# First cross attention: numerator and denominator of a head in one 32-column product, divided and projected in another layout

## The chip, the cores and the metric

The kernel runs on one core of a Trainium2 chip. The metric is device time in microseconds for one launch of the whole program, which computes a small two-layer network; the change touches its first stage only. The stationary operand of a TensorE product is loaded by a weight load (PEld), the moving operand is then streamed by the matmul (PE). VectorE is DVE, ScalarE is ACT, GpSimd is POOL and SyncE, which issues the transfers, is SP.

## The reference

Only the first of the six steps matters here. `x` is normalised (8 samples of 64 tokens, 256 features), and attends to 1024 context rows of 256 features per sample, with 16 heads of 16 features:

```python
rq = (iQ @ Wq.T).reshape(b, q, H, ADIM)          # 8 x 64 x 16 x 16
kv = (iK @ Wkv.T).reshape(b, s, 2, H, ADIM)      # 8 x 1024 x 2 x 16 x 16
scores = einsum('bqhd,bshd->bhqs', rq, rk) / sqrt(ADIM)
scores = where(mask[:, None, :, :], -1e32, scores)
t = relu(scores + nbias[0]); t = t * t
attn = t / (t.sum(-1, keepdims=True) + 1e-32)
o = einsum('bhqs,bshd->bqhd', attn, rv).reshape(b, q, H * ADIM)
x = x + o @ Wo.T
```

The division is made after the product with the values: a numerator (squares times values) over a denominator (sum of the squares).

## The kernel before

`xattn0` writes one instruction stream for each engine; waits on semaphores tie them together, and each engine works through its own list in order. The loop runs over 8 samples `b`, and in each over 4 values of `j`, each with two of the eight 128-row tiles `k` of the context; `n = 8b + k` counts tiles.

TensorE does in one pass of the loop over `j`, in this order: `scores` of the two tiles after the next (`n + 2`, `n + 3`; L468, four 32-row strips of the array side by side), `outputs` of `n` and `n + 1`, and two `piece`s of the keys and values of sample `b + 1` (L181, three fp32r products for one fp32 product). In the last sample there are no pieces. In `outputs` a tile's squares, transposed already (`pr`: context row by (r, c, head of a pair, token)), stream past 32 columns of values, that is two heads (L485, eight matmuls of 128 columns), so that half of each result is the product of one head's squares with the other head's values and is not wanted; and then past 32 columns of ones (L489, four matmuls of 256 columns), which gives the sums. Four matmuls at a time write the four 32-partition quarters of a bank. Each fp32 matmul shows as two matmul records and two weight loads in the trace.

VectorE clamps the scores of a tile (`clamp`, L378), and ScalarE squares them (`squares`, L318), evicts the pieces (`evict`, L307 and L311) and splits the next context (`split`, L298), whose low part GpSimd computes (L286). `scores` of tiles `n + 2`, `n + 3` wait until `clamp` of the pair before has read the same banks. `normalize(b - 1)` on VectorE stands behind the two clamps of `j == 0`: it picks the wanted halves with a 0/1 mask over partitions (`pairmask`, L388 to L392), takes the reciprocal (L394) and multiplies (L395). `limits` and `queries` of the next sample stand at `j == 1` (L366, L368, L361). After the last sample TensorE waits for all of `oT` and does the output projection (L523, eight matmuls), and VectorE adds it to `x` (L428). At the start GpSimd builds the constants, and TensorE waits for `const` before its 20 warming matmuls (L100), which precede the first piece.

```python
pe.wait_ge(const, 3)
core.warm(7, 20)
pe.wait_ge(w_lo, 1)
for n in range(4):
    piece(0, n)
```

Of the kernel before, what the change touches and what calls it, by code (L numbers as in the profile page):

```python
# [188 lines left out]
def xattn0(core, x_d, ctxT_d, maskT_d, wqT_d, wkvT_d, woT_d, nbias_d):  # L189
# [8 lines left out]
    with ExitStack() as ctx:  # L198
# [5 lines left out]
        wo = sb("wo", [P, DC, D])  # L204
# [5 lines left out]
        v = [sb(f"v{i}", [P, KT, D]) for i in range(2)]  # L210
        ones = sb("ones", [P, 32])
# [13 lines left out]
        part, den = sb("part", [P, DC, T]), sb("den", [P, DC, T])  # L225
        num, den_part = sb("num", [P, DC, T]), sb("den_part", [P, DC, T])
        oT = sb("oT", [P, DC, B, T])
# [9 lines left out]
        s_psum, u_ready, p_ready, pv = sem("s_psum"), sem("u_ready"), sem("p_ready"), sem("pv")  # L237
        o_ready, y_psum, x_out = sem("o_ready"), sem("y_psum"), sem("x_out")
# [5 lines left out]
        @block.sync  # L244
        def _(sp):
            def load_context(b):
                for c in range(DC):
                    sp.dma_start(ctxT[:, c, :], ctxT_d[b, c * P:(c + 1) * P, :]).then_inc(ctx_in[c], 16)

            def load_mask(b):  # L250
                sp.dma_start(mask_u8[:], maskT_d[b, :, :].rearrange("p (k t) -> p k t", t=T)).then_inc(mask_in, 16)

            sp.dma_start(wkv[:], wkvT_d.rearrange("(c p) o -> p c o", p=P)).then_inc(wkv_in, 16)
            load_context(0)
            sp.dma_start(x[:], x_d.rearrange("(j p) d -> p j d", p=P)).then_inc(x_in, 16)
# [3 lines left out]
            sp.dma_start(wo[:], woT_d.rearrange("(c p) o -> p c o", p=P)).then_inc(w_in, 16)  # L259
            for b in range(1, B):  # L260
                sp.wait_ge(hi_ready, DC * b)
                sp.wait_ge(lo_ready, DC * b)
                load_context(b)
                sp.wait_ge(mask_read, b)
                load_mask(b)

        @block.gpsimd
        def _(pool):
# [13 lines left out]
            g.memset(ones[:], 1.0).then_inc(const, 1)  # L282
# [7 lines left out]
        def _(act):  # L290
# [9 lines left out]
            def evict(b, n):  # L300
                act.wait_ge(kv_psum, PIECES * b + n + 1)
                bank = core.bank(4 + n % 2)
                if n < 4:
                    c, h = n % 2, n // 2
                    if b >= 2:
                        act.wait_ge(s_psum, KT * (b - 1))
                    A.copy(kT[b % 2][:, c, 512 * h:512 * h + 512], bank).then_inc(kv_ready, 1)  # L307
                else:
                    if b >= 2:
                        act.wait_ge(pv, KT * (b - 1))  # L310
                    A.copy(v[b % 2][:, 2 * (n - 4):2 * (n - 4) + 2, :],  # L311
                           bank.rearrange("p (k d) -> p k d", k=2)).then_inc(kv_ready, 1)
# [24 lines left out]
            act.wait_ge(w_in, 48)  # L337
            squares(0)
            squares(1)
            for b in range(B):  # L340
                for j in range(KT // 2):
                    for i in range(2):
                        n = KT * b + 2 * j + 2 + i
                        if n < LAST:
                            squares(n)
                    if b + 1 < B:
                        evict(b + 1, 2 * j)
                        evict(b + 1, 2 * j + 1)
                    if j == 1 and b + 2 < B:
                        split(b + 2)  # L350

        @block.vector
        def _(dve):
# [29 lines left out]
            def normalize(b):  # L383
                dve.wait_ge(pv, KT * (b + 1))
                half = lambda i: core.bank(6 + b % 2)[:, 256 * i:256 * i + 256].rearrange(
                    "p (c g t) -> p c g t", c=DC, g=2)
                o, d = half(0), half(1)
                step(V.tensor_scalar(part[:], o[:, :, 1, :], pairmask[:, 1:2], None, ALU.mult), False)  # L388
                step(V.tensor_scalar(den_part[:], d[:, :, 1, :], pairmask[:, 1:2], 1e-32, ALU.mult, ALU.add))
                step(V.scalar_tensor_tensor(num[:], o[:, :, 0, :], pairmask[:, 0:1], part[:], ALU.mult,  # L390
                                            ALU.add), False)
                step(V.scalar_tensor_tensor(den[:], d[:, :, 0, :], pairmask[:, 0:1], den_part[:], ALU.mult,  # L392
                                            ALU.add))
                step(V.reciprocal(den[:], den[:]))  # L394
                V.tensor_tensor(oT[:, :, b, :], num[:], den[:], ALU.mult).then_inc(o_ready, 1)  # L395
# [10 lines left out]
            dve.wait_ge(w_in, 48)  # L406
            step(V.tensor_scalar(floor[:], nb[:], -float(HD ** 0.5), None, ALU.mult))
            limits(0)
            dve.wait_ge(const, 3)
# [4 lines left out]
            for b in range(B):  # L414
                for j in range(KT // 2):
# [4 lines left out]
                    if j == 0 and b > 0:  # L420
                        normalize(b - 1)
# [4 lines left out]
            for j in range(2):  # L426
                dve.wait_ge(y_psum, j + 1)
                V.tensor_tensor(x[:, 2 * j:2 * j + 2, :], x[:, 2 * j:2 * j + 2, :],  # L428
                                core.bank(2 + j).rearrange("p (j d) -> p j d", d=D), ALU.add).then_inc(x_out, 1)

        @block.tensor
        def _(pe):
# [40 lines left out]
            def outputs(n):  # L473
                b, k = n // KT, n % KT
                bank = core.bank(6 + b % 2)
                prob = pr[:, n % NP, :].rearrange("p (r c n) -> p r c n", r=RT, c=DC)
# [24 lines left out]
            pe.wait_ge(w_in, 48)  # L501
# [7 lines left out]
            for b in range(B):  # L509
                for j in range(KT // 2):  # L510
# [10 lines left out]
            for j in range(TT):  # L521
                for c in range(DC):
                    last = t.matmul(core.bank(2 + j // 2)[:, D * (j % 2):D * (j % 2) + D],  # L523
                                    oT[:, c, 2 * j:2 * j + 2, :].rearrange("p b q -> p (b q)"), wo[:, c, :],
                                    start=c == 0, stop=c == DC - 1)
                if j % 2:
                    last.then_inc(y_psum, 1)
# [1393 lines left out]
def layout(inputs):  # L1921
# [8 lines left out]
    for n in ("Wq", "Wkv", "Wo"):  # L1930
        a["L0_xattn_" + n] = a["L0_xattn_" + n].T

# [25 lines left out]
```

## Time and profile before

| | |
|---|---|
| median of 3 runs | 1226.44 us (1224.24 to 1230.47) |
| the profiled execution, its own time | 1229.6 us |
| its span | 1227.9 us |
| busy in the span: PE, PEld | 1109.2 us (90%), 930.3 us (76%) |
| busy in the span: DVE, ACT, POOL | 613.6, 578.8, 283.2 us |
| the first cross attention | from 0 to 225 us of the span |

A row of the timeline view has a start and a duration in microseconds, engine, line, operation, tiles and a count of merged records; what stands in square brackets is the engine's idle time before it, and who ended it. Matmul records overlap, so where a merged row's next row starts tells more than its duration.

### The profile page before, as it was taken

To read this page: it belongs to the slowest core of one execution; us is meant where nothing else is said; L and a number is where in the kernel's file an instruction comes from. 1 tells how busy PE (TensorE), PEld (TensorE's weight loads), DVE (VectorE), ACT (ScalarE), POOL (GpSimd) and SP (SyncE) were. 2 spreads that over 40 slices of the span, in tenths; PEclk is the share of its full clock that TensorE was granted. 3 is DMA by queue.
4 is the path that set the end of the run, shared out by engine and by line. 5 is a ranking of instruction groups with operands and counts; after the bars stand their busy time and mean duration, and the time that the engine had idled before them with its cause. 6 is when DMAs were issued, how large, how long until landed. Compare 5 with 4: busy or idle time off the path is not lost. (4 is left out here: it accounts for less than half of the span.)

```text
span 1227.9 us, 21490 instructions
## 1 busy us (share of the span) xinstructions
PE 1109.2 (90%) x8708; PEld 930.3 (76%) x8708; DVE 613.6 (50%) x863; ACT 578.8 (47%) x779; POOL 283.2 (23%) x195
## 2 busy tenths in 40 slices
PE   7999998737899987999999999999999967999998
PEld 6778876434589954798898989889886546888887
DVE  3565566587444435555555555555541266334333
ACT  4666665312366625444444444444430323665563
POOL 2112110205124412111302111131200340343341
PEclk9999999968699978999999999999999977999999
DMA  4111100101023230111112111113000402233220
GB/s 152 45 39 41 72 5 2 39 1 56 1 86 94 60 137 9 60 35 35 35 34 68 34 34 34 34 34 102 0 1 1 152 0 70 69 102 102 68 68 18
DMA packets 47453, 62.39 MB, mean 51 GB/s; under 512 B 5457, under 2 KB 37665, under 8 KB 47393
## 3 DMA queue, kind: packets, MB, share of 16 engines
q1 hardware_dynamic: 47392, 61.52, 15.6%
q8 instruction: 46, 0.75, 0.3%
q14 instruction: 15, 0.12, 0.0%
HBM read 60.99 MB, written 0.52 MB: 50 GB/s over the span
## 5 line engine op out<-in xcount | busy, mean ns | idle before, releaser
L1487 ACT ACTIVATE f_pr<-ps,f_negmax 128x1024 f32<-128x1024 f32 x64 | 71.4, 1116 | 178.8 <-DVE f_negmax L1554 178.8
L181 PE MATMUL ps<-f_pT_hi,f_cN_hi 128*128 128x256 f32 x512 | 145.5, 284 | 2.4 <-DVE f_pT_lo L1549 2.4
L181 PE MATMUL ps<-f_pT_hi,f_cN_lo 128*128 128x256 f32 x512 | 145.0, 283 | 0.0
L181 PE MATMUL ps<-f_pT_lo,f_cN_hi 128*128 128x256 f32 x512 | 144.9, 283 | 0.0
L1549 DVE TENSOR_TENSOR f_pT_lo<-ps,f_pT_hi 128x1024 fp32r<-128x1024 f32 x64 | 78.2, 1222 | 78.7 <-ACT f_pT_hi L1495 78.7
L378 DVE SCALAR_TENSOR_TENSOR a_u<-ps,a_floor,a_cap 128x1024 f32<-128x1024 f32 x64 | 79.2, 1279 | 74.8 <-PE ps L468 74.8
L181 PE MATMUL ps<-e_cT_hi,f_qb_hi 128*128 128x512 f32 x256 | 106.2, 415 | 8.0 <-POOL e_cT_lo L1449 8.0
L959 DVE TENSOR_TENSOR k_h_lo<-k_h,k_h_hi 128x512 fp32r<-128x512 f32 x64 | 58.6, 924 | 101.1 <-ACT k_h_hi L940 101.0
L893 POOL TENSOR_TENSOR k_w_lo<-k_w,k_w_hi 128x1024 fp32r<-128x1024 f32 x32 | 76.5, 2396 | 121.5 <-ACT k_w_hi L920 121.5
L181 PEld LDWEIGHTS ps<-f_pT_hi,f_cN_hi 128*128 128x128 f32 x512 | 98.0, 191 | 4.8 <-DVE f_pT_lo L1549 2.6
L181 PE MATMUL ps<-e_cT_hi,f_qb_lo 128*128 128x512 f32 x256 | 101.1, 395 | 0.0
L181 PE MATMUL ps<-e_cT_lo,f_qb_hi 128*128 128x512 f32 x256 | 100.6, 393 | 0.0
L181 PEld LDWEIGHTS ps<-f_pT_lo,f_cN_hi 128*128 128x128 f32 x512 | 98.1, 192 | 1.6
L318 ACT ACTIVATE a_pr<-a_u,a_nb 128x1024 f32<-128x1024 f32 x64 | 73.7, 1152 | 51.8 <-DVE a_u L378 50.5
L181 PEld LDWEIGHTS ps<-f_pT_hi,f_cN_lo 128*128 128x128 f32 x512 | 98.0, 191 | 0.0
L1554 DVE TENSOR_REDUCE f_negmax<-ps 128x1 f32<-128x1024 f32 x64 | 78.0, 1219 | 36.8 <-PE ps L181 36.8
L1449 POOL TENSOR_TENSOR e_cT_lo<-e_rawT,e_cT_hi 128x512 fp32r<-128x512 f32 x32 | 42.3, 1355 | 220.3 <-ACT e_cT_hi L1471 193.5
L1495 ACT CAST f_pT_hi<-ps 128x1024 fp32r<-128x1024 f32 x64 | 64.8, 1013 | 54.0 <-PE ps L1607 54.0
L936 ACT ACTIVATE k_h<-ps,k_b 128x512 f32<-128x512 f32 x64 | 44.0, 688 | 72.4 <-PE ps L181 72.4
L1607 PE MATMUL ps<-ident,f_pr 128*128 128x128 f32 x512 | 66.6, 273 | 12.6 <-DVE f_pT_lo L1549 11.8
L181 PE MATMUL ps<-k_w_hi,k_h_hi 128*128 128x256 f32 x256 | 73.2, 286 | 0.5 <-DVE k_h_lo L959 0.3
L181 PE MATMUL ps<-k_w_hi,k_h_lo 128*128 128x256 f32 x256 | 72.5, 283 | 0.0
(325 smaller groups left out, 2660.5 us busy)
## 6 DMA issues: line engine op xcount, KB each, us to landing
k_w<-in_L_ffn_W SPq DMA_DIRECT2D x32, 512.0 KB, 3.7
a_ctxT<-in_ctxT SPq DMA_DIRECT2D x16, 512.0 KB, 4.4
d_w<-in_L_ffn_w SPq DMA_DIRECT2D x32, 256.0 KB, 2.7
e_rawT<-in_ctxT SPq DMA_DIRECT2D x8, 1024.0 KB, 4.9
e_raw<-in_ctx SPq DMA_DIRECT2D x8, 1024.0 KB, 5.5
e_wk<-in_L_xattn_w_k SPq DMA_DIRECT2D x1, 1024.0 KB, 6.7
e_wq<-in_L_xattn_w_q SPq DMA_DIRECT2D x1, 1024.0 KB, 8.8
g_wv<-in_L_xattn_w_v SPq DMA_DIRECT2D x1, 1024.0 KB, 7.8
```

Source lines behind the costliest of these rows:

```text
L181: last = nc.tensor.matmul(out, a[i], b[j], start=start and n == 0, stop=stop and n == 2, skip_group_check=skip)
L318: A.activation(pr[:, n % NP, :], u[:, n % NU, :], ACT.Square, bias=nb[:], scale=HD ** -0.5).then_inc(p_ready, 1)
L378: V.scalar_tensor_tensor(u[:, n % NU, :].rearrange("p (r w) -> p r w", r=RT), core.psum[:, 0:2048].rearrange("p (r w) -> p r w", r=RT)[:, ...
L893: self.c.nc.gpsimd.tensor_tensor(lo[:], raw[:], hi[:].bitcast(F32), ALU.subtract).then_inc(self.lo[i], 1)
L936: A.activation(self.h[:, f % self.RH, :], self.c.bank(f % 4), self.func, bias=bias).then_inc(self.h_ready, 1)
L959: V.tensor_tensor(self.hp[1][:, f % self.RG, :], self.h[:, f % self.RH, :], self.hp[0][:, f % self.RG, :].bitcast(F32), ALU.subtract).then ...
L1449: nc.gpsimd.tensor_tensor(cT[1][:, c, cols], rawT[:, c, cols], cT[0][:, c, cols].bitcast(F32), ALU.subtract).then_inc(t_lo, 1)
L1487: nc.scalar.activation(pr[:, p % NPR, :], core.ps[p % 2][:], ACT.Exp, bias=negmax[:, p:p + 1], accum_out=total[:, p:p + 1]).then_inc(exp_r ...
L1495: nc.scalar.copy(pT[0][:, g, :, P * (p % 2):P * (p % 2) + P], core.ps[2][:].rearrange("p (k n) -> p k n", n=P)).then_inc(pT_hi, 1)
L1549: nc.vector.tensor_tensor(pT[1][:, g, :, cols], core.ps[2][:].rearrange("p (k n) -> p k n", n=P), pT[0][:, g, :, cols].bitcast(F32), ALU.s ...
L1554: nc.vector.tensor_reduce(negmax[:, p:p + 1], core.ps[p % 2][:], AX, ALU.max, negate=True).then_inc(max_ready, 1)
L1607: last = nc.tensor.transpose(core.ps[2][:, k * P:(k + 1) * P], pr[:, p % NPR, k * P:(k + 1) * P], core.ident[:])
```

## The change

- `v` holds, per head, 16 columns of values and 16 columns of ones. `outputs` does one matmul of 64 columns per head against these 32 columns (16 matmuls a tile, four at a time). In each 32-partition quarter of the bank 16 partitions then hold numerators and 16 hold the sum, 16 times over. The matmuls against `ones` are gone.
- `numerators` (ScalarE, at `j == 0` of the next sample, ahead of the squares) copies the sample's 128x256 result out of PSUM. `denominators` (TensorE, behind `outputs` of `j == 0`) multiplies it by the 0/1 matrix `spread`, which puts each head's sum beside its numerators, into the other half of the bank. `normalize`, now behind the clamps of `j == 1`, adds 1e-32, takes the reciprocal and multiplies, all of 256 columns.
- `oT` and `wo` have 4 slices of 128 partitions in place of 2, with zero rows in `wo` where `oT` holds no numerators. The projection is 16 matmuls in place of 8. Three of its four row blocks (`project(0)` to `project(2)`) stand in the last sample's loop, where there are no pieces.
- GpSimd fills `spread`, all of `wo` and the ones columns of both `v` buffers at the start, and TensorE and VectorE wait for `const` 6 in place of 3. `wo` is loaded by four transfers behind a wait for its fill. The squares and the products with `Wq` no longer wait for `wo`.

```diff
-        wo = sb("wo", [P, DC, D])
+        wo = sb("wo", [P, 4, D])
...
-        v = [sb(f"v{i}", [P, KT, D]) for i in range(2)]
-        ones = sb("ones", [P, 32])
+        v = [sb(f"v{i}", [P, KT, H, 2 * HD]) for i in range(2)]
+        spread = sb("spread", [P, 4, 32])
...
+            sp.wait_ge(const, 4)
+            for j in range(4):
+                sp.dma_start(wo[32 * j:32 * j + HD, :, :], woT_d[HD * j:HD * j + HD, :].rearrange(
+                    "d (i o) -> d i o", o=D)).then_inc(wo_in, 16)
...
-            g.memset(ones[:], 1.0).then_inc(const, 1)
+            step(g.memset(spread[:], 0.0))
+            g.affine_select(out=spread[:], in_=spread[:], compare_op=ALU.not_equal, fill=1.0, base=-HD,
+                            pattern=[[-32, 4], [0, 32]], channel_multiplier=1).then_inc(const, 1)
+            g.memset(wo[:], 0.0).then_inc(const, 1)
+            for i in range(2):
+                g.memset(v[i][:, :, :, HD:2 * HD], 1.0).then_inc(const, 1)
...
+            def numerators(b):
+                act.wait_ge(pv, KT * (b + 1))
+                if b >= 1:
+                    act.wait_ge(o_ready, b)
+                A.copy(num[:], core.bank(6 + b % 2)[:, 0:256].rearrange("p (h t) -> p h t", t=T)
+                       ).then_inc(num_ready, 1)
...
+                    if j == 0 and b > 0:
+                        numerators(b - 1)
...
-                dve.wait_ge(pv, KT * (b + 1))
...
+                dve.wait_ge(den_psum, b + 1)
+                step(V.tensor_scalar(den[:], core.bank(6 + b % 2)[:, 256:512].rearrange("p (h t) -> p h t", t=T), 1e-32,
+                                     None, ALU.add))
                 step(V.reciprocal(den[:], den[:]))
                 V.tensor_tensor(oT[:, :, b, :], num[:], den[:], ALU.mult).then_inc(o_ready, 1)
...
-            dve.wait_ge(const, 3)
+            dve.wait_ge(const, 6)
...
-                    if j == 0 and b > 0:
+                    if j == 1 and b > 0:
                         normalize(b - 1)
...
                 for c in range(DC):
-                    for j in range(4):
-                        quarter = slice(32 * j, 32 * j + 32)
-                        t.matmul(bank[quarter, P * c:P * c + P], v[b % 2][:, k, P * c + 32 * j:P * c + 32 * j + 32],
-                                 prob[:, j, c, :], start=k == 0 and c == 0, stop=k == KT - 1,
-                                 skip_group_check=True)
-                for j in range(4):
-                    last = t.matmul(bank[32 * j:32 * j + 32, 2 * P:4 * P], ones[:],
-                                    prob[:, j, :, :].rearrange("p c n -> p (c n)"), start=False, stop=k == KT - 1, skip_group_check=True)
+                    for g in range(2):
+                        col = T * (2 * c + g)
+                        for j in range(4):
+                            last = t.matmul(bank[32 * j:32 * j + 32, col:col + T], v[b % 2][:, k, 8 * c + 2 * j + g, :],
+                                            prob[:, j, c, g, :], start=k == 0 and c == 0 and g == 0,
+                                            stop=k == KT - 1, skip_group_check=True)
                 last.then_inc(pv, 1)
 
-            pe.wait_ge(const, 3)
+            def denominators(b):
+                pe.wait_ge(num_ready, b + 1)
+                t.matmul(core.bank(6 + b % 2)[:, 256:512], spread[:].rearrange("p j m -> p (j m)"),
+                         num[:].rearrange("p h t -> p (h t)"), start=True, stop=True).then_inc(den_psum, 1)
+
+            def project(j):
+                pe.wait_ge(o_ready, 2 * j + 2)
+                for i in range(4):
+                    last = t.matmul(core.bank(4 + j // 2)[:, D * (j % 2):D * (j % 2) + D],
+                                    oT[:, i, 2 * j:2 * j + 2, :].rearrange("p b q -> p (b q)"), wo[:, i, :],
+                                    start=i == 0, stop=i == 3)
...
+            pe.wait_ge(const, 6)
             core.warm(7, 20)
...
+                    if j == 0 and b > 0:
+                        denominators(b - 1)
                     if b + 1 < B:
                         piece(b + 1, 2 * j)
                         piece(b + 1, 2 * j + 1)
-            pe.wait_ge(o_ready, B)
...
+                    else:
+                        if j == 0:
+                            pe.wait_ge(wo_in, 64)
+                            pe.wait_ge(kv_ready, PIECES * B)
+                        if j < 3:
+                            project(j)
+            denominators(B - 1)
+            project(TT - 1)
```

TensorE at `j == 0` of the second sample (`b = 1`), before, from the scores to the first pieces:

```order
L468 MATMUL ps<-a_qd,a_kT 128x128 x16
L485 MATMUL ps<-a_pr,a_v 32x128 x8
L489 MATMUL ps<-a_pr,a_ones 32x256 x4
L485 MATMUL ps<-a_pr,a_v 32x128 x8
L489 MATMUL ps<-a_pr,a_ones 32x256 x4
L181 MATMUL ps<-a_ctx_hi,a_wkv_hi 128x512
```

The same place in the changed kernel, where L479 is the line of the scores, L497 that of the products of a head and L504 that of the product with `spread`:

```order
L181 MATMUL ps<-a_wkv_hi,a_ctx_lo 128x256
L479 MATMUL ps<-a_qd,a_kT 128x128 x16
L497 MATMUL ps<-a_pr,a_v 32x64 x32
L504 MATMUL ps<-a_num,a_spread 128x256
L181 MATMUL ps<-a_ctx_hi,a_wkv_hi 128x512
```

24 matmuls of 128 and 256 columns have become 32 of 64, and one product of 256 columns stands between them and the pieces.

VectorE in the same sample before, from the clamps of `j == 2` of the sample ahead to those of `j == 2` of this one, where `normalize` stands between the clamps of `j == 0` and of `j == 1`:

```order
L378 SCALAR_TENSOR_TENSOR a_u<-ps,a_floor,a_cap 128x1024 x6
L388 TENSOR_SCALAR a_part<-ps,a_pairmask 128x128
L389 TENSOR_SCALAR a_den_part<-ps,a_pairmask 128x128
L390 SCALAR_TENSOR_TENSOR a_num<-ps,a_pairmask,a_part 128x128
L392 SCALAR_TENSOR_TENSOR a_den<-ps,a_pairmask,a_den_part 128x128
L394 RECIPROCAL a_den<-a_den 128x128
L395 TENSOR_TENSOR a_oT<-a_num,a_den 128x2x64
L378 SCALAR_TENSOR_TENSOR a_u<-ps,a_floor,a_cap 128x1024 x2
L366 TENSOR_SCALAR a_big<-a_mask_u 128x512
L368 TENSOR_SCALAR a_cap<-a_big,a_floor 128x2048
L361 TENSOR_TENSOR a_qd<-a_qT,a_pairmask 128x128 x2
```

And in the changed kernel:

```order
L396 SCALAR_TENSOR_TENSOR a_u<-ps,a_floor,a_cap 128x1024 x8
L403 TENSOR_SCALAR a_den<-ps 128x256
L405 RECIPROCAL a_den<-a_den 128x256
L406 TENSOR_TENSOR a_oT<-a_num,a_den 128x4x64
L384 TENSOR_SCALAR a_big<-a_mask_u 128x512
L386 TENSOR_SCALAR a_cap<-a_big,a_floor 128x2048
L379 TENSOR_TENSOR a_qd<-a_qT,a_pairmask 128x128 x2
```

The six instructions of `normalize` have become three of twice the width, and they, `limits` and `queries` now form one block without a clamp between.

TensorE at the end of the changed stage, in the last sample (L510 is the line of `project`; before, all of the projection stood behind the last `outputs`):

```order
L479 MATMUL ps<-a_qd,a_kT 128x128 x16
L497 MATMUL ps<-a_pr,a_v 32x64 x32
L504 MATMUL ps<-a_num,a_spread 128x256
L510 MATMUL ps<-a_wo,a_oT 128x256 x4
L479 MATMUL ps<-a_qd,a_kT 128x128 x16
L497 MATMUL ps<-a_pr,a_v 32x64 x32
L510 MATMUL ps<-a_wo,a_oT 128x256 x4
```

A quarter of the projection, four matmuls, follows the products of each of `j` 0 to 2.

## Rows read from the trace of the kernel before

**Rows 1.** Busy time of each engine, PEclk granted, in two stretches of the stage

```profile
100.00:150.00 50.00, 50.00 (x856) 40.27 (x852) 29.86 (x38) 30.88 (x37) 9.53 (x5) 1.00 0.14 49
...
220.00:222.00 2.00, 2.00 (x7) 1.56 (x6) 0.63 (x1) 0.00 (x0) 0.00 (x0) 0.51 0.00 0
```

**Rows 2.** Groups of the stage by form: count, busy us, mean ns of one

```profile
L485 PE MATMUL ps<-a_pr,a_v 128*32 128x128 f32 x1024 | 41.0, 278 | 0.8 <-ACT a_pr L318 0.7
L489 PE MATMUL ps<-a_pr,a_ones 128*32 128x256 f32 x512 | 39.8, 383 | 0.0
```

**Rows 3.** Timeline of PE, one pass of the loop over j (sample 3)

```profile
101.12 0.61 PE L489 MATMUL ps<-a_pr,a_ones 128*32 128x256 f32 x8
101.55 0.62 PE L485 MATMUL ps<-a_pr,a_v 128*32 128x128 f32 x16
101.99 0.61 PE L489 MATMUL ps<-a_pr,a_ones 128*32 128x256 f32 x8
102.53 0.38 PE L181 MATMUL ps<-a_wkv_hi,a_ctx_hi 128*128 128x256 f32 x1
...
105.57 1.17 PE L468 MATMUL ps<-a_qd,a_kT 32*128 32x128 f32 x32
```

**Rows 4.** Timeline of DVE, one sample and the clamps behind it

```profile
106.81 2.48 DVE L378 SCALAR_TENSOR_TENSOR a_u<-ps,a_floor,a_cap 128x1024 f32<-128x1024 f32 x2 [3.54 <-PE ps L468]
109.20 0.34 DVE L388 TENSOR_SCALAR a_part<-ps,a_pairmask 128x128 f32<-128x128 f32 x1
...
112.78 2.48 DVE L378 SCALAR_TENSOR_TENSOR a_u<-ps,a_floor,a_cap 128x1024 f32<-128x1024 f32 x2 [1.02 <-PE ps L468]
115.17 0.42 DVE L366 TENSOR_SCALAR a_big<-a_mask_u 128x512 f32<-128x512 uint8 x1
...
116.83 0.48 DVE L361 TENSOR_TENSOR a_qd<-a_qT,a_pairmask 128x128 f32<-128x128 f32 x2
118.75 2.48 DVE L378 SCALAR_TENSOR_TENSOR a_u<-ps,a_floor,a_cap 128x1024 f32<-128x1024 f32 x2 [1.44 <-PE ps L468]
```

**Rows 5.** Timeline of ACT, the squares in the first pass of the same sample

```profile
108.13 2.35 ACT L318 ACTIVATE a_pr<-a_u,a_nb 128x1024 f32<-128x1024 f32 x2 [1.87 <-DVE a_u L378]
```

**Rows 6.** Timeline of PE, later stages: products of 16 and of 8 columns

```profile
306.52 1.66 PE L1277 MATMUL ps<-c_vd,c_pT 128*64 128x16 f32 x29 [1.10 <-ACT c_pT L1187]
...
337.15 1.92 PE L819 MATMUL ps<-d_gate_w,c_mlaT 128*128 128x8 f32 x16 [1.04 <-PEq L1110]
```

**Rows 7.** Groups of DVE, ACT and POOL by form, as prices

```profile
L394 DVE RECIPROCAL a_den<-a_den 128x128 f32<-128x128 f32 x8 | 7.6, 953 | 0.3
L1219 DVE RECIPROCAL c_sm<-c_sm 128x16 f32<-128x16 f32 x4 | 1.0, 253 | 0.1
L1841 DVE TENSOR_TENSOR h_y<-ps,h_bo 128x256 f32<-128x256 f32 x4 | 1.6, 424 | 2.2 <-PE ps L1888 2.2
L307 ACT COPY a_kT<-ps 128x512 f32<-128x512 f32 x32 | 18.5, 578 | 15.1 <-PE ps L181 15.1
L1157 POOL MEMSET c_vd<- 128x1024 f32 x1 | 1.0, 951 | 0.0
L286 POOL TENSOR_TENSOR a_ctx_lo<-a_ctxT,a_ctx_hi 128x1024 fp32r<-128x1024 f32 x14 | 33.2, 2394 | 136.0 <-ACT a_ctx_hi L298 136.0
```

**Rows 8.** Timeline of PE and DVE, the last sample and the projection

```profile
201.41 1.17 PE L468 MATMUL ps<-a_qd,a_kT 32*128 32x128 f32 x32
...
215.00 0.64 PE L485 MATMUL ps<-a_pr,a_v 128*32 128x128 f32 x16
...
216.14 0.35 DVE L388 TENSOR_SCALAR a_part<-ps,a_pairmask 128x128 f32<-128x128 f32 x1 [2.38 <-PE ps L489]
...
218.76 5.41 PE L523 MATMUL ps<-a_wo,a_oT 128*128 128x256 f32 x16 [2.69 <-DVE a_oT L395]
...
224.21 0.69 DVE L428 TENSOR_TENSOR resid<-resid,ps 128x512 f32<-128x512 f32 x1 [2.15 <-PE ps L523]
```

**Rows 9.** Timeline of PE, the start of the program

```profile
2.78 7.40 PE L100 MATMUL ps<-ident 128*128 128x128 f32 x40 [2.78 <-POOL a_ones L282]
9.94 0.48 PE L181 MATMUL ps<-a_ctx_hi,a_wkv_hi 128*128 128x512 f32 x1
```

More of the change, by code:

```diff
@@ L224, in xattn0 @@
         pr = sb("pr", [P, NP, H * T])
-        part, den = sb("part", [P, DC, T]), sb("den", [P, DC, T])
-        num, den_part = sb("num", [P, DC, T]), sb("den_part", [P, DC, T])
-        oT = sb("oT", [P, DC, B, T])
+        num, den = sb("num", [P, 4, T]), sb("den", [P, 4, T])
+        oT = sb("oT", [P, 4, B, T])
         x_in, wkv_in, w_in, const = sem("x_in"), sem("wkv_in"), sem("w_in"), sem("const")
@@ L237, in xattn0 @@
         s_psum, u_ready, p_ready, pv = sem("s_psum"), sem("u_ready"), sem("p_ready"), sem("pv")
+        num_ready, den_psum, wo_in = sem("num_ready"), sem("den_psum"), sem("wo_in")
         o_ready, y_psum, x_out = sem("o_ready"), sem("y_psum"), sem("x_out")
@@ L310, in evict @@
                         act.wait_ge(pv, KT * (b - 1))
-                    A.copy(v[b % 2][:, 2 * (n - 4):2 * (n - 4) + 2, :],
-                           bank.rearrange("p (k d) -> p k d", k=2)).then_inc(kv_ready, 1)
+                    A.copy(v[b % 2][:, 2 * (n - 4):2 * (n - 4) + 2, :, 0:HD],
+                           bank.rearrange("p (k h d) -> p k h d", k=2, h=H)).then_inc(kv_ready, 1)
+            def numerators(b):
[4 more added lines that the diff above has]
+                       ).then_inc(num_ready, 1)
             def squares(n):
@@ L336, in _ @@
                 A.copy(qT[:, c, :], core.bank(2 + c)).then_inc(q_ready, 1)
-            act.wait_ge(w_in, 48)
+            act.wait_ge(w_in, 32)
             squares(0)
@@ L350, in _ @@
                         split(b + 2)
+            numerators(B - 1)
         @block.vector
@@ L383, in normalize @@
             def normalize(b):
-                dve.wait_ge(pv, KT * (b + 1))
[L385 to L393, printed above, removed]
+                dve.wait_ge(den_psum, b + 1)
+                step(V.tensor_scalar(den[:], core.bank(6 + b % 2)[:, 256:512].rearrange("p (h t) -> p h t", t=T), 1e-32,
+                                     None, ALU.add))
                 step(V.reciprocal(den[:], den[:]))
@@ L482, in outputs @@
                 for c in range(DC):
-                    for j in range(4):
-                        quarter = slice(32 * j, 32 * j + 32)
-                        t.matmul(bank[quarter, P * c:P * c + P], v[b % 2][:, k, P * c + 32 * j:P * c + 32 * j + 32],
-                                 prob[:, j, c, :], start=k == 0 and c == 0, stop=k == KT - 1,
-                                 skip_group_check=True)
-                for j in range(4):
-                    last = t.matmul(bank[32 * j:32 * j + 32, 2 * P:4 * P], ones[:],
-                                    prob[:, j, :, :].rearrange("p c n -> p (c n)"), start=False, stop=k == KT - 1, skip_group_check=True)
-                last.then_inc(pv, 1)
-            pe.wait_ge(const, 3)
+                    for g in range(2):
[4 more added lines that the diff above has]
+                                            stop=k == KT - 1, skip_group_check=True)
+                last.then_inc(pv, 1)
+            def denominators(b):
[8 more added lines that the diff above has]
+                                    start=i == 0, stop=i == 3)
+                if j % 2:
+                    last.then_inc(y_psum, 1)
+            pe.wait_ge(const, 6)
             core.warm(7, 20)
@@ L500, in _ @@
                 piece(0, n)
-            pe.wait_ge(w_in, 48)
+            pe.wait_ge(w_in, 32)
             for c in range(DC):
@@ L519, in _ @@
                         piece(b + 1, 2 * j + 1)
-            pe.wait_ge(o_ready, B)
[L521 to L527, printed above, removed]
+                    else:
[6 more added lines that the diff above has]
+            project(TT - 1)
 def store_x(core, out_d):
@@ L1929, in layout @@
     a["maskT"] = mask.reshape(B, T, KT, P).transpose(0, 3, 2, 1).reshape(B, P, KT * T)
-    for n in ("Wq", "Wkv", "Wo"):
+    for n in ("Wq", "Wkv"):
         a["L0_xattn_" + n] = a["L0_xattn_" + n].T
+    a["L0_xattn_Wo"] = a["L0_xattn_Wo"].T.reshape(2, 4, 2, 16, D).transpose(1, 3, 0, 2, 4).reshape(64, 4 * D)
     a["L0_ffn_q_w"] = a["L0_ffn_q_w"].reshape(D, 16, 2, 8)[:, :, 0, :].reshape(D, P)
```

7 lines of the change are left out of this document (3 added, 4 removed).

## Prediction

> **What bounds the kernel now.** I read first the busy times by stretch: between 100 and 150 us TensorE is busy all of 50.00 us at a granted clock of 1.00, VectorE 29.86 and ScalarE 30.88 us [rows 1]. So in the loop every column that TensorE no longer streams is time, until another engine's loop becomes longer. The timeline shows one pass of the loop over j [rows 3]: the two tiles' products go 0.43 us (ones), 0.44 us (values), and so on, and the next scores start at 105.57. The clamps of neighbouring passes start 5.97 us apart [rows 4], and of the four passes of a sample two hold key pieces and two value pieces; I take 5.97 for the first and second pass and 6.01 for the other two (scores at 105.57, 6.01 behind those of the pass before, by the same pattern). A sample takes 23.96 us. VectorE's slack is seen in the square brackets: it waits 3.54 us for the scores ahead of the clamps of a first pass, but only 1.02 behind normalize and 1.44 behind limits and queries [rows 4]. It has slack in each pass, and little in two of them.
>
> **Products of a tile.** Matmuls of 128 and of 256 columns take 278 and 383 ns [rows 2]: 105 ns for 128 columns, 0.82 ns a column. 16 records of the values take 0.44 us [rows 3], that is four rounds of four side by side at 110 ns, 105 of them columns and about 5 fixed. 8 records against ones take 0.43 us, two rounds of 216. After the change a tile has 16 matmuls, so 32 records of 64 columns, eight rounds. A round of 64 columns is 52 + 5 = 57 ns if nothing else limits it, so a tile takes 0.46 in place of 0.87 us: 0.41 less, 0.83 a pass, 3.3 a sample.
>
> What else could limit a round is the weight load. Sixteen products of 8 columns with a 128-column load take 1.92 us, so 111 ns apiece without the last one's latency; 29 records of 16 columns with a 64-column load take 1.66 us, some 52 to 57 ns apiece [rows 6]. Both are the load: about 0.85 ns a column. A load of 32 columns is then 27 ns, under 57, and if the four quarters load side by side as they stream it stays hidden. The rate at which records follow is the unproven part. The densest that these rows show is 16 records in 0.44 us, 27 ns apiece as a mean, and the change wants 14 ns. Ends: 14 ns (0.41 saved a tile) and 27 ns (nothing saved). I take 14, because the 27 is explained by the columns streamed: the ones, with twice the columns, come at 54 ns a record, and the 0.82 ns a column holds for both.
>
> The Trainium skill speaks against this: "TensorE: Matmul & The Clock Gate", section "Wait — 56ns, not 53.3ns?", says that start-to-start of matmuls never falls below about 25 ns however few the columns. Taken for the whole engine that makes a tile 0.80 us and saves 0.07 in place of 0.41, and the time would be that of the milder form of the first rival; the rows here do not contradict it, since their mean is 27. The page's section on small matmuls packed into one array gives about 4 ns between starts of matmuls in different tiles of the array, which would leave my 57 ns round alone.
>
> **The product with spread.** One matmul of 256 columns, two records of 256 × 0.82 = 0.21 us: 0.43 us in the first pass of each sample from the second on. Its load comes with a change of layout that the pieces pay for now. It waits for numerators on ScalarE, a 128x256 copy, between 0 and the 0.578 us of 512 columns [rows 7]; I take 0.36. It stands ahead of squares that wait 1.87 us for VectorE today [rows 5], so it is hidden; uncovered it would cost 0.36 a sample.
>
> **VectorE in the second pass.** Normalize moves behind the clamps of j == 1, ahead of limits and queries. Its price: the addition from PSUM of 256 columns 0.42 (as L1841); the reciprocal, from 253 ns for 16 columns and 953 for 128, 6.25 ns a column, 1.75 for 256; the multiplication at most 0.42; three gaps of 0.04 [rows 7]. That is 2.7 us; before, it was six instructions in 2.55. The reciprocal's ends are 0.95 (no growth) and 1.9 (doubled).
>
> Count from the start of the scores of the second pass. The clamps start 1.24 later (105.57 to 106.81) and the next instruction starts 2.39 after that [rows 3, 4], at 3.63. Normalize ends at 6.35, limits and queries take 2.14 (115.17 to 116.83 + 0.48) and end at 8.5. The clamps of the third pass, whose scores are ready at 6.4, wait for that and end at 10.95, and the scores of the fourth pass, which write the same banks, start about 0.14 later, at 11.1. TensorE would be there at 5.14 + 5.18 = 10.3 (5.97 and 6.01 less 0.83). It stands for 0.8 us, with the products and pieces queued behind the scores. The squares of the third pass end near 12.3, before the products behind those scores want them at 12.2 to 12.7, and nothing of the lateness reaches the pass after. So samples 1 to 6 (from 0) each gain 3.3 − 0.43 − 0.8 = 2.1 us, 12.4 in all, and sample 0, which has neither, 3.3.
>
> **The last sample.** There are no pieces, and the loop from scores to clamp to scores sets the pace. Before, the last products start 13.6 us and VectorE's first instruction behind them 14.7 us after the sample's first scores (201.41, 215.00, 216.14) [rows 8]. After, TensorE's first pass holds scores 1.1, products 1.0, spread 0.43 and project(0), four matmuls of 256 columns, 8 × 0.21 = 1.7 us: with the switches 4.4. The clamps of the second pass then run from 5.7 to 8.1 and normalize to 10.8; those of the third start at 10.8 and end at 13.2, the squares of the last tile at 14.5, and its products end at 15.2. Project(1) and project(2) lie under those waits. 0.5 us is lost.
>
> **The tail.** Before, 8.8 us from 216.14 to the end of the addition, 224.90 [rows 8]. After: numerators 0.36, the spread product until VectorE sees it 0.85, normalize 2.7, project(3) with eight records 1.7 to 3.4 and 0.3 of latency, addition 0.69 and 0.2 of handing over: 6.8 to 8.5. The clock decides: the old projection's 16 records take 5.41 us, since the granted clock was 0.51 from 220 to 222, that is 1.2 GHz after TensorE had waited 2.69 us for VectorE [rows 1, 8]. The new wait is longer. I take 7.7: 1.1 gained.
>
> **The start.** TensorE's warming starts at 2.78, ended by the fill of ones, and its 40 records end just ahead of the first piece at 9.94 [rows 9]. It now waits for fills of spread (about 0.7 with its steps), wo and both v. GpSimd's fill of 1024 columns takes 0.95 us, 0.83 ns a column with about 0.1 fixed [rows 7]: wo 0.95, and each v has 8 × 16 × 16 = 2048 columns, 1.8. Warming starts near 7.8, 5.0 us later. It may run somewhat faster, as the clock's steps fall elsewhere in it; the first piece comes 4.0 to 5.0 us later, I take 4.5. Nothing hides it: VectorE and ScalarE wait for these pieces too. Ends for the two v fills: 1.8 each, or 2.39 for every 1024 columns as in GpSimd's subtraction [rows 7], 4.8 each, since each writes runs of 16 columns. I take 1.8, as a fill reads nothing. The transfers of wo behind SyncE's new wait, and the next context queued behind them, have the whole first sample before they are wanted.
>
> **Sum.** −3.3 − 12.4 + 0.5 − 1.1 + 4.5 = −11.8, against the profiled execution's 1229.6: 1217.8. That execution lies 3.2 above the median 1226.4, so the median is forecast at 1214.6. Stages behind this one keep their time.
>
> **Rivals.**
> First, ending slower: TensorE can't take records closer than the 27 ns shown. A tile stays at 0.87 us, VectorE's block causes no stall (two passes are 12.0, over 11.1), and the new work remains: spread 7 × 0.43 = 3.0, last sample +1.8 (its first pass becomes 5.4 and the third 1.0 later still), tail −1.1, start +4.5: +8.2, 1234.6. It turns slower from 23 ns a record on, where 60 tiles × 0.13 us pay for the rest. For it: no row is denser. Against it: the mean follows the columns. A milder form, a rate halfway between 23 and 27, saves 0.07 us on each of some 60 tiles and gives +4.0: 1230.4.
> Second, the fills of v at 4.8 us each: +6.0, 1220.6. For it the strided runs of 16; against it nothing but the simpler operation.
> Third, VectorE's block is short enough or TensorE's gain small enough that no stall appears: six times 0.8 back, 1209.8. For it only the reciprocal's lower end; against it two sizes on one line.
>
> **Chances.** Forecast 0.58; first rival 0.10, its milder form 0.08; second 0.12; third 0.07; anything else 0.05. Within the forecast, the start (±0.5), the tail (±0.9), the stall (±0.3, six times) and a low-clock window that may fall elsewhere (±1) make about ±4. The range, 1208 to 1226, takes in the forecast, the second and the third. A measurement tells some 0.5% (6.1 us) from no change: below 1220.3 is faster, above 1232.6 slower. Faster 0.72 (the forecast, the third, over half of the second), same 0.17, slower 0.11.
>
> **What would show it.** In the changed profile: 32 records of 64 columns in 0.46 us a tile (0.80 or more: the first rival); first piece at 14 to 15 us and fills of v of 1.8 us; sample period 21.9 us; an idle TensorE of 0.8 us ahead of the fourth pass's scores, ended by the clamp; reciprocals of 1.75 us; the stage ending near 213. It is wrong in its main term if the period stays above 23, and in its side terms if the stage's end and 8 periods don't fit together.

## The result

| | kernel before | changed kernel |
|---|---|---|
| median | 1228.45 us (1224.24 to 1231.46) | 1243.26 us (1242.54 to 1246.52) |
| the profiled execution, its span | 1229.6, 1227.9 us | 1246.5, 1244.8 us |
| granted clock, mean of the span | 0.954 | 0.941 |
| the stage's last addition ends | 224.90 us | 241.49 us |

The ratio is 1.0128, with an interval of 1.0089 to 1.0167: the change makes the kernel some 1.3% slower. 1214.6 was forecast, and the range ended at 1226. The stage ends 16.6 us later and the span 16.9 us later, so what stands behind the stage kept its time (1003.0 and 1003.3 us), as forecast. The loss lies in the stage.

The start. The timeline of PE of the changed kernel answers to [rows 9]:

```profile
7.71 6.66 PE L100 MATMUL ps<-ident 128*128 128x128 f32 x40 [7.71 <-POOL a_v L290]
14.13 0.47 PE L181 MATMUL ps<-a_ctx_hi,a_wkv_hi 128*128 128x512 f32 x1
```

The groups of the stage by form answer to [rows 2, 7] (count, busy us, mean ns of one, idle time before):

```profile
L497 PE MATMUL ps<-a_pr,a_v 128*32 128x64 f32 x2048 | 38.5, 231 | 1.1 <-ACT a_pr L333 1.1
...
L294 POOL TENSOR_TENSOR a_ctx_lo<-a_ctxT,a_ctx_hi 128x1024 fp32r<-128x1024 f32 x14 | 37.8, 2723 | 141.5 <-ACT a_ctx_hi L306 141.5
...
L379 DVE TENSOR_TENSOR a_qd<-a_qT,a_pairmask 128x128 f32<-128x128 f32 x16 | 25.7, 1644 | 8.3 <-ACT a_qT L351 8.3
...
L405 DVE RECIPROCAL a_den<-a_den 128x256 f32<-128x256 f32 x8 | 14.0, 1753 | 0.3
...
L386 DVE TENSOR_SCALAR a_cap<-a_big,a_floor 128x2048 f32<-128x2048 f32 x8 | 10.3, 1286 | 0.3
...
L290 POOL MEMSET a_v<- 128x2048 f32 x2 | 3.5, 1804 | 0.0
...
L406 DVE TENSOR_TENSOR a_oT<-a_num,a_den 128x256 f32<-128x256 f32 x8 | 3.4, 426 | 0.3
...
L403 DVE TENSOR_SCALAR a_den<-ps 128x256 f32<-128x256 f32 x8 | 3.3, 416 | 3.4 <-PE ps L504 3.4
```

One row doesn't fit its size. The diff moves `queries` (L379) in VectorE's list, but not what it computes, and its sixteen instructions take 1644 ns in the mean, in the kernel before 284 (two in 0.48 us in [rows 4]). GpSimd's subtraction of the low part of the context (L294) takes 2723 ns, 2394 in [rows 7]. Nothing in either was edited.

The timelines of DVE, POOL and PE of the changed kernel show where this happens. They are of sample 2 (counted from 0) and answer to [rows 3, 4]:

```profile
96.15 0.41 DVE L403 TENSOR_SCALAR a_den<-ps 128x256 f32<-128x256 f32 x1
96.60 1.75 DVE L405 RECIPROCAL a_den<-a_den 128x256 f32<-128x256 f32 x1
98.39 0.43 DVE L406 TENSOR_TENSOR a_oT<-a_num,a_den 128x256 f32<-128x256 f32 x1
98.73 0.42 DVE L384 TENSOR_SCALAR a_big<-a_mask_u 128x512 f32<-128x512 uint8 x1
99.19 1.29 DVE L386 TENSOR_SCALAR a_cap<-a_big,a_floor 128x2048 f32<-128x2048 f32 x1
100.39 4.84 DVE L379 TENSOR_TENSOR a_qd<-a_qT,a_pairmask 128x128 f32<-128x128 f32 x2
105.15 2.46 DVE L396 SCALAR_TENSOR_TENSOR a_u<-ps,a_floor,a_cap 128x1024 f32<-128x1024 f32 x2
```

```profile
99.40 5.68 POOL L294 TENSOR_TENSOR a_ctx_lo<-a_ctxT,a_ctx_hi 128x1024 fp32r<-128x1024 f32 x2 [21.65 <-ACT a_ctx_hi L306]
```

```profile
98.75 1.10 PE L497 MATMUL ps<-a_pr,a_v 128*32 128x64 f32 x64
99.78 0.38 PE L181 MATMUL ps<-a_wkv_hi,a_ctx_hi 128*128 128x256 f32 x1
...
107.76 2.09 PE L479 MATMUL ps<-a_qd,a_kT 32*128 32x128 f32 x32 [4.88 <-DVE a_u L396]
109.78 1.54 PE L497 MATMUL ps<-a_pr,a_v 128*32 128x64 f32 x64
111.26 0.39 PE L181 MATMUL ps<-a_wkv_hi,a_ctx_hi 128*128 128x256 f32 x1
```

VectorE's block runs without a gap from normalize to the next clamp, as forecast, but its last two instructions, the queries, last 4.84 us: they run while GpSimd does its two subtractions (99.40 to 105.08). The clamps behind them end late, and TensorE stands 4.88 us ahead of the scores of the fourth pass. Behind that wait it works at the lower of its two clocks, as the stretch from 108 to 110 us shows (columns as in [rows 1]):

```profile
108.00:110.00 2.00, 2.00 (x41) 1.77 (x45) 0.09 (x1) 1.76 (x3) 0.00 (x0) 0.50 0.65 266
```

PEclk is 0.50, that is 1.2 GHz: the scores take 2.02 us to the next row in place of 1.10, the products 1.48 in place of 1.03. In the waits of PE between 30 and 240 us the wait for the clamp, 5.1 us in 3 times before, is

```profile
PE ps L479 <- DVE a_u L396: 27.5, 7, 4.9
```

In [rows 4] queries end at 117.31. In that sample of the kernel before, the first of GpSimd's subtractions starts 1.9 us later. ScalarE's `split` starts it (timelines of POOL and ACT):

```profile
119.22 4.76 POOL L286 TENSOR_TENSOR a_ctx_lo<-a_ctxT,a_ctx_hi 128x1024 fp32r<-128x1024 f32 x2 [19.20 <-ACT a_ctx_hi L298]
...
118.10 1.99 ACT L298 CAST a_ctx_hi<-a_ctxT 128x1024 fp32r<-128x1024 f32 x2
```

The same of the changed kernel, timeline of ACT:

```profile
98.27 2.00 ACT L306 CAST a_ctx_hi<-a_ctxT 128x1024 fp32r<-128x1024 f32 x2
```

Counted from the start of the second pass's clamps (112.78 before, 93.76 after), two things moved. Normalize puts the queries 2.6 us further back, from 4.05 to 6.63 us. The split comes 0.8 us earlier, at 4.51 in place of 5.32 us, which is about what the products of a pass got shorter by. The 2.6 us alone are more than the distance of 1.9 us; the 0.8 us alone would have left 1.1. Sample 6 has no context to split; it serves as a control inside the same execution (timelines of DVE and PE):

```profile
205.85 1.75 DVE L405 RECIPROCAL a_den<-a_den 128x256 f32<-128x256 f32 x1
...
209.64 0.48 DVE L379 TENSOR_TENSOR a_qd<-a_qT,a_pairmask 128x128 f32<-128x128 f32 x2
```

```profile
212.66 1.17 PE L479 MATMUL ps<-a_qd,a_kT 32*128 32x128 f32 x32 [0.53 <-DVE a_u L396]
```

**The ledger**, by the start of `a_cap` (L386 after, L368 before), one in each sample but the last: first at 48.27 us (before 43.74: +4.5, start); the next 23.6 us later (before 23.96: −0.4); five more at 27.32 apart (before 23.96: +16.8); from the last, 208.44, to the end of the stage 33.05 us (before 37.4: −4.35). The sum is +16.6. The five periods were forecast at 21.9, so 5 × 5.4 = 27 us of the miss of 28.7 us stand there. A period is made up as: the one without a collision, forecast with a stall of 0.8, has 0.5, hence 21.6; 4.36 for the queries; 0.92 and 0.45 for scores and products at 1.2 GHz: 27.3.

### The profile page after: what moved, and what is told of

Read it like the earlier page. It is cut to its first block and busy times, and to the rows that moved or that the text cites. A ratio compares the mean times of both kernels' runs of the same rounds, so it can differ in the third digit from the quotient of the medians.

```text
span 1244.8 us, 22578 instructions
## 1 busy us (share of the span) xinstructions
PE 1098.5 (88%) x9252; PEld 934.8 (75%) x9252; DVE 638.3 (51%) x839; ACT 580.2 (47%) x787; POOL 292.7 (24%) x199
## 5 line engine op out<-in xcount | busy, mean ns | idle before, releaser
L100 PE MATMUL ps<-ident 128*128 128x128 f32 x208 | 34.2, 340 | 47.1 <-ACT b_cs L670 20.8
```

## Experiments

The theory P: a VectorE instruction of `queries` can't run while one of GpSimd's subtractions does; it waits for the one in flight. The rivals (the first two are "Theory L" below): the longer block alone sets the period; the denser traffic of TensorE and ScalarE slows VectorE's instructions, whatever GpSimd does; or the later start or the products lose the time. Each kernel below is the changed one with the edit shown, apart from the two that say otherwise.

**Normalize back in the first pass.** The block is short again, and queries come early.

```diff
-                    if j == 1 and b > 0:
+                    if j == 0 and b > 0:
                         normalize(b - 1)
```

> The changed kernel with normalize back behind the clamps of the first pass, where the kernel before had it. Theory P: queries end before the subtractions start as in the kernel before, and the block of the second pass no longer stalls TensorE at all: period 23.96 - 3.3 + 0.43 = 21.1 us, some 5 us less than with queries moved alone, time about 1211. Theory L: also gains, since the block is cut in two, but queries' own duration would stay above 284 ns because the traffic is as dense as in the changed kernel.

Measured: 1211.2 us, ratio 0.9846 (0.9821 to 0.9871). Timeline of DVE, then of POOL:

```profile
89.66 1.29 DVE L386 TENSOR_SCALAR a_cap<-a_big,a_floor 128x2048 f32<-128x2048 f32 x1
90.86 0.49 DVE L379 TENSOR_TENSOR a_qd<-a_qT,a_pairmask 128x128 f32<-128x128 f32 x2
```

```profile
92.46 4.75 POOL L294 TENSOR_TENSOR a_ctx_lo<-a_ctxT,a_ctx_hi 128x1024 fp32r<-128x1024 f32 x2 [16.25 <-ACT a_ctx_hi L306]
```

Queries end 1.1 us before GpSimd starts and take 0.49 us, GpSimd's two are back at 4.75, and the period is 21.00 us. All of the loss and more comes back. This takes away the collision and the long block both; the next run parts them.

**The split a pass later.** The long block stays, GpSimd moves.

```diff
-                    if j == 1 and b + 2 < B:
+                    if j == 2 and b + 2 < B:
                         split(b + 2)
```

> The changed kernel with one edit: ScalarE splits the context after next in the third pass, not in the second, so GpSimd's two subtractions start one pass later; VectorE's order is untouched. Theory P: queries no longer meet a subtraction, 284 ns, period 22 us, time about 1217. Theory L: VectorE's block is the same, so nothing moves, 1243.

Measured: 1218.94 us, 0.9911 (0.9882 to 0.994), period 22.39. Timelines of DVE, POOL and PE:

```profile
93.16 1.29 DVE L386 TENSOR_SCALAR a_cap<-a_big,a_floor 128x2048 f32<-128x2048 f32 x1
94.37 0.49 DVE L379 TENSOR_TENSOR a_qd<-a_qT,a_pairmask 128x128 f32<-128x128 f32 x2
```

```profile
100.41 4.74 POOL L294 TENSOR_TENSOR a_ctx_lo<-a_ctxT,a_ctx_hi 128x1024 fp32r<-128x1024 f32 x2 [17.65 <-ACT a_ctx_hi L306]
```

```profile
97.39 1.17 PE L479 MATMUL ps<-a_qd,a_kT 32*128 32x128 f32 x32 [0.54 <-DVE a_u L396]
...
104.43 1.10 PE L497 MATMUL ps<-a_pr,a_v 128*32 128x64 f32 x64 [0.70 <-issue]
```

So the long block costs TensorE 0.54 us a sample, as against 0.8 forecast, and 4.88 only with the collision. The rival of the long block falls, and with it that of the traffic: in the same block, beside the same work of TensorE, the pair of queries takes 0.49 us. The 0.70 us stands ahead of the first products of the next sample, which wait for the last eviction of values. On ScalarE split (99.27 to 101.28) now stands ahead of the squares, and these ahead of that eviction, which ends at 104.33. So the 0.70 us is most likely the price of the moved split; that was read, not tested.

**Queries ahead of normalize**, limits behind it, in the second pass.

```diff
+                    if j == 1 and b + 1 < B:
+                        queries(b + 1)
                     if j == 1 and b > 0:
                         normalize(b - 1)
                     if j == 1 and b + 1 < B:
                         limits(b + 1)
-                        queries(b + 1)
```

> The changed kernel with one edit: in the second pass of a sample VectorE does queries of the next sample ahead of normalize and limits, not behind them. Theory P (port): a VectorE instruction with two SBUF inputs that meets a GpSimd subtraction waits until that ends. Moved up, queries are over before GpSimd starts: their mean falls from 1644 ns to about 284, the sample period from 27.3 to 22 us, and the time from 1243.3 by five samples of 5.3 us to about 1217. Theory L (length): VectorE's block is simply too long or its instructions are slowed by the denser traffic of TensorE and ScalarE, whatever GpSimd does: the same instructions in the same block, so queries stay slow and the time stays near 1243.

Measured: 1229.33 us, 0.9998 (0.9978 to 1.0017), 12 us above what P expected. Queries are back at 284 ns. Timelines of POOL, DVE and PE:

```profile
96.74 5.71 POOL L294 TENSOR_TENSOR a_ctx_lo<-a_ctxT,a_ctx_hi 128x1024 fp32r<-128x1024 f32 x2 [19.43 <-ACT a_ctx_hi L306]
```

```profile
96.47 0.42 DVE L384 TENSOR_SCALAR a_big<-a_mask_u 128x512 f32<-128x512 uint8 x1
96.93 3.30 DVE L386 TENSOR_SCALAR a_cap<-a_big,a_floor 128x2048 f32<-128x2048 f32 x1
```

```profile
102.76 2.09 PE L480 MATMUL ps<-a_qd,a_kT 32*128 32x128 f32 x32 [2.54 <-DVE a_u L396]
```

The collision went to another instruction. `a_cap`, with one tensor input, now starts 0.2 us behind GpSimd's first subtraction and takes 3.30 us in place of 1.29. In the changed kernel it had started 0.2 us ahead of GpSimd (99.19 and 99.40) and kept its 1.29, while GpSimd's two took 5.68 in place of 4.75. P was too narrow: not only instructions with two tensor inputs are held up, and the one that starts first keeps its time.

Not all of the 12 us is the collision's own. The five periods behind a slow `a_cap` are 25.1, 26.4, 25.2, 23.6 and 23.6 us, at a mean granted clock of 0.93, 0.87, 0.93, 1.00 and 1.00. So a collision costs some 2 us of the period by itself, and up to 2.8 us more where the clock falls behind the wait.

**Queries with one tensor input**, at the changed kernel's place, by the form of `a_cap`.

```diff
-                    V.tensor_tensor(qd[b % 2][:, c, :, :], bc(qT[:, c, b * T:(b + 1) * T], 1, HR),
-                                    bc(pairmask[:], 2, T), ALU.mult).then_inc(qd_ready, 1)
+                    for h in range(HR):
+                        last = V.tensor_scalar(qd[b % 2][:, c, h, :], qT[:, c, b * T:(b + 1) * T],
+                                               pairmask[:, h:h + 1], None, ALU.mult)
+                    last.then_inc(qd_ready, 1)
```

> The changed kernel with queries written as four multiplications by a column of the mask (one SBUF tensor and a scalar for each partition) in place of two products of two SBUF tensors, in the same place. If only a second tensor input brings the wait for GpSimd: four instructions of 0.15 to 0.2 us, period 22 us, time about 1217. If every fast fp32 form from SBUF to SBUF takes the port as well: the first of the four waits for a subtraction and at least one other too, and the time stays between 1235 and 1245.

Measured: 1248.58 us, 1.0148 (1.0122 to 1.0174), some 4 us above the range expected for the second case. The four instructions take, in the timeline of DVE,

```profile
101.42 5.02 DVE L380 TENSOR_SCALAR a_qd<-a_qT,a_pairmask 128x64 f32<-128x64 f32 x4
```

and over the kernel one of them takes from 240 to 2398 ns, with a median of 247: in the block shown two of the four take the wait, one for each subtraction. One tensor input does not spare an instruction that reads and writes SBUF in this form.

The Trainium skill, "SBUF — State Buffer", section "Who interferes with whom", has both halves: VectorE and GpSimd share a pair of ports under an exclusive lock that whoever starts first holds for its whole instruction, and VectorE wants it for two SBUF inputs against a GpSimd instruction that reads SBUF, and for one input in the two-port modes that `tensor_scalar` can enter. The trace agrees: 2.42 us for a query, 3.30 for `a_cap` when GpSimd is first, 1.29 when it is first itself, and then 5.68 for GpSimd's two.

**The kernel before, its queries one pass later**: the collision without the change.

```diff
                     if j == 1 and b + 1 < B:
                         limits(b + 1)
+                    if j == 2 and b + 1 < B:
                         queries(b + 1)
```

> The kernel before with one edit: queries move from the second pass to the third, behind its clamps, where they meet GpSimd's subtractions (95.26 to 100.0 us in the sample read, clamps ending at 97.2). Theory P: queries rise from 284 ns to 1.2 to 2.5 us each, in a kernel whose TensorE traffic is that of before; they are over by about 100.4, ahead of the next clamps at 100.8, so the time stays within 0.5% of before. Theory L: they stay at 284 ns.

Measured: 1234.73 us, 1.0039 (1.002 to 1.0058), period 24.73 against 23.96. Timelines of DVE and PE:

```profile
99.83 3.04 DVE L361 TENSOR_TENSOR a_qd<-a_qT,a_pairmask 128x128 f32<-128x128 f32 x2
104.20 2.48 DVE L378 SCALAR_TENSOR_TENSOR a_u<-ps,a_floor,a_cap 128x1024 f32<-128x1024 f32 x2 [1.33 <-PE ps L469]
```

```profile
102.97 1.17 PE L469 MATMUL ps<-a_qd,a_kT 32*128 32x128 f32 x32 [0.70 <-ACT a_v L311]
```

GpSimd's two run from 97.91 to 102.72. The pair of queries takes 3.04 us in place of 0.48 in the kernel before too: the first takes 0.65, as it comes late in the first subtraction, the second 2.48. The slowing isn't a property of the new layout. The queries end at 102.87 and not at 100.4 as expected, and the 0.77 us of the period comes by a path that I had overlooked: the scores of the fourth pass are the next sample's first tiles and need these queries. They start 0.10 us behind their end, and TensorE stands 0.70 us ahead of them. The view puts that wait down to a ScalarE copy, but this ended at 101.57.

**GpSimd in halves.** The changed kernel, each subtraction of 1024 columns made as two of 512.

```diff
-                    g.tensor_tensor(ctx_lo[b % 2][:, c, :], ctxT[:, c, :], ctx_hi[b % 2][:, c, :].bitcast(F32),
-                                    ALU.subtract).then_inc(lo_ready, 1)
+                    for h in range(2):
+                        cols = slice(512 * h, 512 * h + 512)
+                        last = g.tensor_tensor(ctx_lo[b % 2][:, c, cols], ctxT[:, c, cols],
+                                               ctx_hi[b % 2][:, c, cols].bitcast(F32), ALU.subtract)
+                    last.then_inc(lo_ready, 1)
```

> The changed kernel with each of GpSimd's subtractions of 1024 columns cut into two of 512, in the same place; VectorE's order is untouched. Theory P, in its exact form (a VectorE instruction waits for the one GpSimd instruction in flight and then takes its turn): each query waits for at most one half, 1.2 us, so a pair takes 2.0 to 2.7 us in place of 4.84, the sample period falls from 27.3 to about 25 us and the time from 1243.3 to about 1231. Rival: VectorE is held off until GpSimd has no subtraction left, whatever their size: a pair stays near 4.8 us and the time at 1243.

Measured: 1228.35 us, 0.9991 (0.9971 to 1.001), with a mean of 24.97 us over the five periods with a collision. Timelines of POOL and DVE:

```profile
97.02 6.02 POOL L296 TENSOR_TENSOR a_ctx_lo<-a_ctxT,a_ctx_hi 128x512 fp32r<-128x512 f32 x4 [19.29 <-ACT a_ctx_hi L309]
```

```profile
98.01 2.67 DVE L382 TENSOR_TENSOR a_qd<-a_qT,a_pairmask 128x128 f32<-128x128 f32 x2
100.60 2.46 DVE L399 SCALAR_TENSOR_TENSOR a_u<-ps,a_floor,a_cap 128x1024 f32<-128x1024 f32 x2
```

A pair of queries takes 2.67 in place of 4.84 us, one of them 1.38. VectorE waits for the instruction in flight, so the wait has the length of GpSimd's instruction; it isn't held off until GpSimd has no subtraction left. The clamps that read PSUM start in the middle of GpSimd's four (97.02 to 103.04) and take 2.46, as ever. This speaks for a lock and against engines that merely slow each other down: then the queries' time wouldn't follow the length of GpSimd's instruction.

**The start**, by itself: warming waits for fewer fills.

```diff
-            pe.wait_ge(const, 6)
+            pe.wait_ge(const, 2)
             core.warm(7, 20)
...
+            pe.wait_ge(const, 6)
             pe.wait_ge(w_in, 32)
```

> The changed kernel, but TensorE waits only for the first two constants ahead of its warming products, and for all six ahead of the products with Wq. It prices the fills at the start: the first piece returns from 14.1 to about 10 us and the time falls by 4 to 4.5 us to 1239. If something else (transfers, VectorE) held the start, it falls less.

Measured: 1242.81 us, 1.0094 (1.0064 to 1.0124). The first piece starts at 10.28 in place of 14.13, and the stage ends at 237.88 in place of 241.49. So the stage gives 3.6 us and the profiled spans 4.0, but the medians only 0.45 in place of the 4 to 4.5 expected, with intervals that overlap; where the rest stays has no cause shown. The start came as forecast (4.5 us), so it isn't the cause of the miss.

**Both**: normalize in the first pass and the early start.

> The changed kernel with normalize in the first pass and the early start together. Theory P and the prices above add: 1211 - 4.3 = 1207, 1.7% below the kernel before. If the two share a cause, less.

Measured: 1202.96 us, 0.9778 (0.975 to 0.9806), 4 us less than expected. This beats both kernels. The stage ends at 203.85, 21 us before that of the kernel before; the period is 21.0. The run with normalize alone moved ends its stage at 207.02, so the early start gives 3.2 us there.

**The same with the whole projection at the end**, which undoes the change's early part.

```diff
-                        if j < 3:
-                            project(j)
+                        pass
             denominators(B - 1)
-            project(TT - 1)
+            for j in range(TT):
+                project(j)
```

> The kernel with normalize in the first pass and the early start, with all four row blocks of the projection behind the last normalize. It prices the early part of the projection: three blocks of eight records go to the tail at 1.7 to 3.4 us each, so 5 to 9 us more than with them early, less 0.7 in the last sample's first pass where TensorE then waits for the clamp; 1212 to 1215.

Measured: 1210.93 us, 0.9843 (0.9809 to 0.9876). The stage ends at 207.04, so the early projection is worth 3.2 us of the stage, less than the 5 to 9 expected. The medians lie 8.0 us apart; the rest stands outside of the stage and has no cause shown here. What follows the stage varies from 997.2 to 1005.7 us between the profiled executions of these kernels, so a difference of a few us between medians is less sure than one between two stages.

## Why the prediction was wrong

**The step that failed** is "limits and queries take 2.14 (115.17 to 116.83 + 0.48) and end at 8.5", in VectorE in the second pass. The price came from a row of the old place [rows 4], where GpSimd was idle. At the new place the two took 6.5 us (98.73 to 105.23), because GpSimd's subtractions were running, and ended 4.4 us later than their old price gives. The working asked when VectorE would be there and who would wait for it, and never what else ran at that moment. POOL's timeline of the kernel before was needed, and the 1.9 us between the end of queries and the subtraction stood in it. Step by step:

- **What bounds the kernel** held: with the collision gone every column less on TensorE was time.
- **Products** held. Two tiles' 64 records take 1.03 us to the next row (98.75 to 99.78). Before, the last eight records took 0.54 to the pieces' row and 0.43 to another product's [rows 3], so 0.11 of it is the switch: 16 rounds of 57 ns, 14 ns a record. The rival with 27 ns and its milder form fall for four column groups side by side. The Trainium skill, "TensorE: Matmul & The Clock Gate", section "Wait — 56ns, not 53.3ns?", has no start-to-start below about 25 ns; taken for the whole engine that doesn't hold here, and the measurement decides.
- **The spread product** held: TensorE never waited for it in the loop (one wait of 0.5, at the end).
- **The last sample** held: 15.1 us from its first scores (217.82) to the numerators (232.95), where its products were forecast to end at 15.2.
- **The reciprocal**, addition and multiplication: 1753, 416 and 426 ns, forecast 1.75, 0.42 and at most 0.42.
- **The stall** was mechanically right (same engine, same place, ended by the clamp), 0.54 where nothing collides against 0.8, and 4.88 with the collision. The third rival, no stall, fell as well.
- **The period** was forecast at 21.9; 22.39 with the split moved, 27.32 in the changed kernel.
- **The start**: fills of `v` 1.80 us each, warming at 7.71 (7.8 forecast), first piece +4.2 (4.5). The second rival fell.
- **The tail**: 8.5 us (numerators 232.95, end 241.49) against 7.7. The clock was the open point, and it was the low one (0.50 granted from 238 to 240 us, behind a wait of 2.77): project(3) took 3.63 us, where 1.7 to 3.4 and 0.3 of latency had been allowed. The timelines of ACT, PE and DVE of the changed kernel, against [rows 8]:

```profile
232.95 0.37 ACT L326 COPY a_num<-ps 128x256 f32<-128x256 f32 x1 [0.77 <-PE ps L497]
...
237.13 3.63 PE L510 MATMUL ps<-a_wo,a_oT 128*128 128x256 f32 x8 [2.77 <-DVE a_oT L406]
...
240.80 0.69 DVE L439 TENSOR_TENSOR resid<-resid,ps 128x512 f32<-128x512 f32 x1 [3.13 <-PE ps L510]
```

- **What would show it wrong** worked: "if the period stays above 23" pointed to the term at once.
- **The rivals** that would have ended slower were all on TensorE. The one that came true needed two facts, that queries move back and that GpSimd starts behind the same pass's split; both stood in the trace and the diff. "Anything else" had 0.05, too little for a block of VectorE moved by 2.6 us beside an engine never looked at.

## What to carry to other kernels

When an instruction moves in time, look at what the other engines do at its new time, and price it there. Here `queries` and `a_cap`, which read and write SBUF only, waited for up to the whole of a GpSimd subtraction wherever they came while it ran; the clamps, which read PSUM, didn't. A unit of work that is cheap at one place can so be the dearest at another. Moving either of the two by one pass gave the time back (1211.2 and 1218.94 us in place of 1243.26), and cutting GpSimd's work into shorter instructions gave about half of it (1228.35). The change itself was worth having (0.9778 with normalize and one wait moved): a bad result of a change of many parts says little of its main part.

## What the runs showed of the hardware

- VectorE waits for the GpSimd subtraction in flight: 2.42 us a query against 0.28, with subtractions of 2.39 alone; 1.38 with halves, which take 1.28 alone. Each query behind another catches a subtraction of its own.
- Whoever starts first keeps its time. An `a_cap` 0.2 us ahead of GpSimd takes 1.29 us and GpSimd is late; 0.2 us behind, it takes 3.30.
- The clamp, which reads PSUM and one tensor in SBUF, isn't held up: 2.46 us a pair in the middle of GpSimd's halves, 2.48 without them.
- Four column groups of 32 columns take records of 64 columns at 14 ns apiece, with their weight loads hidden.
- Reciprocal of fp32 goes by size: 953 ns for 128 columns, 1753 for 256.
